# One whole value product after both score pairs, in place of two halves between them, in a fused attention kernel on one core

## What is computed

```python
def _attend(q, k, v):
    attn = jnp.einsum('bhnd,bhsd->bhns', q, k) * SCALE
    attn = jax.nn.softmax(attn, axis=-1)
    o = jnp.einsum('bhns,bhsd->bhnd', attn, v)
    ...
```

## Time and profile before

| what | value |
|---|---|
| median of 3 executions | 3727.86 us (3714.53 to 3728.5) |
| profiled execution, its own time | 3726.77 us |
| span in its trace | 3724.2 us |
| TensorE busy in the span | 3381.6 us |
| ScalarE busy | 2297.7 us |
| VectorE busy | 2203.2 us |
| mean granted TensorE clock | 0.965 |

### The profile page before, as it was taken

How to read it: one execution, slowest core, us unless ns; L and a number is a source line. 1 busy time by engine, 2 the same in 40 slices (tenths; PEclk the granted TensorE clock), 3 DMA queues, 4 the chain that set the end, 5 groups by cost and what they waited for, 6 DMA issues and landing times.

```text
span 3724.2 us, 59944 instructions
## 1 busy us (share of the span) xinstructions
PE 3381.6 (91%) x21985; PEld 1991.7 (53%) x21985; DVE 2203.2 (59%) x3645; ACT 2297.7 (62%) x3983; POOL 870.2 (23%) x578
## 2 busy tenths in 40 slices
PE   8999998898999888998898889988998899899988
PEld 6777766434644564446434744465446443564465
DVE  3323324794387456953884559636955487549654
ACT  2333333787578655875786558765874578658864
POOL 0322322103500421024103410061024100340051
PEclk8989989999999999999999999999999999999999
DMA  5011012010100001111010011100100101000100
GB/s 183 1 36 34 2 36 87 8 15 26 39 9 12 13 13 57 16 29 39 4 16 14 12 57 11 33 24 17 15 18 12 57 8 25 24 28 11 22 13 13
DMA packets 226984, 101.18 MB, mean 27 GB/s; under 512 B 159951, under 2 KB 210322, under 8 KB 226582
## 3 DMA queue, kind: packets, MB, share of 16 engines
q1 hardware_dynamic: 201734, 77.21, 8.3%
q10 hardware_dynamic: 24976, 20.15, 1.7%
HBM read 79.31 MB, written 9.96 MB: 24 GB/s over the span
## 4 chain that ended last, share of the span: by engine, by line
PE 75%; DVE 13%; ACT 7%; issue 2%; POOL 2%; DMA 1%; SPq 0%; ACTq 0%; DVEq 0%; POOLq 0%
PE ps L734 72%; DVE mxh L1789 4%; ACT probs L1468 2%; PE ps L1182 2%; DVE ctxk L1738 2%; DVE ow L1821 1%; DVE tok L1524 1%; PE ps L1043 1%; DVE small L1508 1%; DVE x L1755 1%; POOL hidl L1917 1%; DVE mx L1786 1%; ACT ow L1477 1%; ACT qs L1437 1%; POOL small L1845 1%
## 5 line engine op out<-in xcount | busy, mean ns | idle before, releaser
L1468 ACT ACTIVATE probs<-ps 128x512 f32<-128x512 f32 (+1 forms) x2176 | 1216.1, 640 | 257.0 <-PE ps L734 212.9
L1789 DVE TENSOR_REDUCE mxh<-ps 128x2 f32<-128x1024 f32 x1024 | 1217.1, 1217 | 151.8 <-PE ps L734 148.7
L734 PE MATMUL ps<-probs,v 128*32 128x256 f32 (+2 forms) x7616 | 720.9, 450 | 30.7 <-ACT ow L1477 24.4
L734 PE MATMUL ps<-ks,qs 64*128 64x512 f32 x2048 | 483.8, 481 | 63.5 <-DVE mxh L1789 34.3
L734 PE MATMUL ps<-qs,ks 64*128 64x512 f32 x2048 | 449.1, 415 | 6.7 <-DVE mxh L1789 6.1
L734 PEld LDWEIGHTS ps<-ks,qs 64*128 64x128 f32 x2048 | 192.6, 183 | 424.4 <-issue 302.9
L734 PEld LDWEIGHTS ps<-qs,ks 64*128 64x128 f32 x2048 | 250.6, 184 | 177.1 <-ACT probs L1468 150.0
L1909 POOL TENSOR_TENSOR hT<-hT,tok 128x512 f32<-128x512 f32 (+1 forms) x32 | 40.9, 1279 | 1250.5 <-DMA tok<-weights_of_outputs 1250.5
L734 PEld LDWEIGHTS ps<-probs,v 128*32 128x32 f32 (+1 forms) x7616 | 151.2, 107 | 309.1 <-ACT probs L1468 230.7
L734 PE MATMUL ps<-hT,slot 128*128 128x512 f32 x448 | 237.3, 663 | 21.4 <-issue 8.5
L1786 DVE TENSOR_REDUCE mx<-ps 128x4 f32<-128x312 f32 x384 | 165.9, 477 | 143.0 <-PE ps L734 139.7
(11 more groups left out here) (226 smaller groups left out, 5911.2 us busy)
## 6 DMA issues: line engine op xcount, KB each, us to landing
qs<-mx SPq DMA_DIRECT2D x896, 0.5 KB, 2.0
slot<-in_L_w SPq DMA_DIRECT2D x8, 1024.0 KB, 9.7
slot<-in_L_fc_w SPq DMA_DIRECT2D x8, 1024.0 KB, 5.2
hT<-ow SPq DMA_DIRECT2D x48, 128.0 KB, 2.7
tok<-weights_of_outputs SPq DMA_DIRECT2D x192, 32.0 KB, 1.8
xin<-in_x ACTq DMA_DIRECT2D x5, 1024.0 KB, 5.9
x_after_block<-x ACTq DMA_DIRECT2D x20, 256.0 KB, 2.4
xin<-x_after_block SPq DMA_DIRECT2D x5, 1024.0 KB, 5.5
```

The costliest lines, as they stand in the source:

```text
L734: return pe.matmul(out, lhsT, rhs, start=start, stop=stop)
L1468: ins = act.activation(dst, src, ACT.Exp, scale=SCALE)
L1789: dve.tensor_reduce(mxh[:, z, t, j // 2, j % 2, :], ps[:, a:a + 2, :], AX.X, ALU.max, negate=True).then_inc(dve_done, M.add(dve_done, name))
```

## The change

After the change the order within a unit that still has maxima to issue is: the first score pair, all its `A` steps, the second score pair, and then the value product of unit u - 2, whole, for every kt. Units 52 and later keep their order: first pair, whole value product, second pair. The eighth kt's product still comes at the end of its unit.

```diff
             unit = units[u - lag] if u >= lag else None
-            in_halves = unit is not None and unit[2] > 0 and taken < len(maxima)
+            maxima_first = u < end and taken < len(maxima)
+            if maxima_first:
+                more(lead + min(3 * (u + 1), 2 * (u + 1) + 4))
+                put(tag, *[("S",) + units[u] + (j,) for j in range(2, GH)])
             if unit is not None:
-                put(tag, ("PVh" if in_halves else "PV",) + unit)
-            if u < end:
-                if in_halves:
-                    more(lead + min(3 * (u + 1), 2 * (u + 1) + 4) - 1)
+                put(tag, ("PV",) + unit)
+            if u < end and not maxima_first:
                 put(tag, *[("S",) + units[u] + (j,) for j in range(2, GH)])
-            if in_halves:
-                put(tag, ("PV",) + unit)
             if unit is not None and unit[2] == NT - 1:
                 put(tag, ("O",) + unit[:2])
                 turn = unit[:2] if unit[0] == GROUPS - 1 else None
-            if u < end:
-                more(lead + min(3 * (u + 1), 2 * (u + 1) + 4))
...
-                            ins = mm(ps[32 * j:32 * j + 32, b, cs], v[0:kw, kt, GH * g + j, :],
-                                     probs[0:kw, u, j, cs], kt == 0, cross or kt == NT - 1 and kind == "PV")
-                        if kind == "PVh":
-                            continue
+                            ins = mm(ps[32 * j:32 * j + 32, b, :], v[0:kw, kt, GH * g + j, :],
+                                     probs[0:kw, u, j, :], kt == 0, cross or kt == NT - 1)
```

More of the change, by code:

```diff
@@ L296 @@
 PASS = pass_schedule()
-HALVED = {k for k in PASS if k[1] == "PVh"}
 def by_dve(tag, kind, *step):
@@ L1151, in _ @@
                             ins = mm(ps[:, b, :], ks[r, h // 2, kt * P:(kt + 1) * P], qs[r, h // 2, half])
-                    elif kind in ("PV", "PVh"):
+                    elif kind == "PV":
                         g, n, kt = step[1:]
[L1154 to L1157, removed]
+                        u = buffer_of(name)
                         b, act_was = 7, []
```

## The result

| | before | after |
|---|---|---|
| median | 3724.23 us (3714.53 to 3728.5, 4 runs) | 3792.54 us (3777.94 to 3797.19, 4 runs) |
| profiled execution, span | 3724.2 us | 3795.4 us |
| TensorE busy | 3381.6 us | 3467.9 us |
| mean granted TensorE clock | 0.965 | 0.954 |

The kernel became slower: ratio 1.018, 95% interval 1.0161 to 1.0198. The forecast was 3760 us with a range from 3735 to 3785; the time lies above it. The medians are 68.3 us apart and the two spans 71.2, since the execution of after that was profiled is the longest of its four (3797.19 us).

What follows compares the result with a forecast made beforehand. TensorE's list was taken to bound the unit at 2.475 us, DVE close behind. Terms 2.4 + 2.3 - 0.7 = 4.0 us a self attention, 32 for eight, gave 3760 us, range 3735 to 3785.

Steps and rivals of the forecast that it cites:

- A slower clock: TensorE's clock falling to its lower level at the new gaps, longest some 0.6 us; given no chance.
- The loop of the bank: Units 4 to 51: fourth score waits for the first's bank; 0.53 + 0.65 + 0.42 + 0.99 makes a unit 2.6 us.
- Copies: ACT's copies of bank 7, mid-stretch: 20.86 us apart for eight units, against 20.48 before.
- units 4 to 51: The six (g, n) of mid-stretch, +0.38 us each: 2.3 us more a self attention.
- The reductions' loop: Mid-stretch: second `A` waits for DVE to free its banks; 4.97 us for two units, 2.49 each, below 2.6.
- Unit 52: First unit without `A`: its wait for a bank of the last reductions goes, -0.7 us a self attention.
- Units 0 to 3, waits: Bank waits beside `V` in units 1 and 2, 1.9 us, and DVE waiting, 0.5: together 2.4 a self attention.
- The sum: 2.4 + 2.3 - 0.7 = 4.0 us a self attention, 32 for eight; median 3760 us.
- ends: Terms outside mid-stretch, at units 0 to 3 and unit 52: between 1 and 3 us in the range.
- Gain: Bank's wait stays hidden, units of 2.49 us: -3.6 a self attention, 3699 us; chance of over 0.5% faster 0.08.
- No change: Loop 0.05 to 0.1 us too long, or units 0 to 3 free: within 18.6 us of before; chance 0.14.
- Slower still: Bank's and DVE's waits add up instead of overlapping, unit 2.7 us: 38 us more, 3798; chance 0.08.

Runs made afterwards that it cites:

- The first experiment: New order from unit 4 on, old order in units 0 to 3, against the kernel before: 3747.01 us, ratio 1.0061.
- the fourth experiment: New order from unit 4 on, plus self-attention exponentials over 256 of 512 columns, value products reading those twice: 3699.86 us in one execution.
- the fifth: New order from unit 4 on, but value products for kt > 0 cut into two halves back to back: 3744.47 us in one execution.
- the second experiment: New order in units 0 to 3 alone, the rest as in the kernel before: 3767.2 us, ratio 1.010.

## Why the prediction went wrong

**The step that failed is the clock.** I wrote "A slower clock is no rival that I give a chance: the longest new gap is some 0.6, and with gaps of 0.52 and more the rows stand at 1.00 now." The runs show that low clock in the units 0 to 3 costs 28 us: 68 us at the lower level where the kernel before has none. Filling one of two gaps there, with nothing else changed, takes 48 of the 68 away and gives back some 21 us. The fault was in the comparison. The gap of 0.52 in the earlier trace rows comes once in 20 us of otherwise dense work. The new gaps come in units 0 to 3, where TensorE waits 1.18 for DVE already, and the next gap now follows it within a unit. I held the clock's 1.00 for an answer to how long a gap may be; it had answered that for one place. A price could have been had from the rows: a stretch of units 0 to 3 is 17.36 long, so each tenth of clock missing in it is about 1.7 an attention and 14 in the whole, and a rival at 0.8 (a level known only now) would have stood at 3788.

**The loop of the bank held.** Unit 2.61, forecast 2.6; its four terms 0.53, 0.65, 0.43, 1.00 against 0.53, 0.65, 0.42, 0.99. Copies 20.93 apart, forecast 20.86; units 4 to 51 cost 2.68, forecast 2.3, the difference being 48 units at 0.01. The first experiment shows this part alone, the fourth that it goes when only half of the bank is read, the fifth that order and not size makes it.

**The reductions' loop held too**: forecast as the next bound at 8 x 2.49 = 19.9, measured 20.03 in the fourth experiment.

**Unit 52**: forecast -0.7, measured -0.68.

**Units 0 to 3, waits**: forecast 2.4, measured 2.28, as what the other terms leave. Of its parts, 1.9 beside `V` and 0.5 for DVE, no run gives either by itself.

**The sum.** 34.2 without the clock, forecast 32: 3726.8 + 34 is 3761. On it lie 28 of clock in the units 0 to 3, which the second experiment shows together with the waits there (40.7 in all for four units of 64), and some 9 elsewhere. The range had a slip of its own: a loop of 2.65 and ends of 3 give 3.7 an attention more than the 4.0 forecast, so 3790 and not 3785; the median lies above that too.

**The rivals.** Gain fell: the bank's wait shows in every unit. No change fell. *Slower still* named a time near the true one, 3798, for another reason; its waits don't add up, since units are 2.61 and not 2.7.

**Open.** Why, of eight attentions with one list of instructions, two have 3.4 us at the lower level and three have 13.7 is not settled, nor is where the gaps must lie to bring the clock down: with `V` behind the pairs it fell in all eight, with one gap filled in five. Gaps near one another are not the whole answer either: ahead of unit 0 the kernel before waits 1.18 and then 0.60 within 2.3 us (690.76 to 693.05), at a clock of 1.00. Shown is that filling a gap took most of it away; filling both was not tried. The 9 us in the rest are mostly the clock by the estimate above, but why it was low there more often is open: each kernel was profiled in one execution, and low stretches lie elsewhere in each. The median of after rests on four runs within 19 us, which is wider than that remainder.

## What to carry to other kernels

Before a second use of a ring of banks is moved nearer to the first, write down what must pass between (here 0.53 + 0.65 = 1.18 us from score to free bank) and what the old order had there: work that seemed badly placed (half a product) was the cover, and saving 0.35 us of TensorE's work in a unit bought a wait of 0.5. A filler belongs where a bank or a copy is late, as the product between third and fourth score at kt = 0, which gave 1.1%. Where new gaps come into a stretch in which TensorE waits already, give the lower clock a price before it is held constant: the new waits here are 13.4 / 8 = 1.7 us an attention, and the clock took up to 24.1 - 19.0 = 5.1 on top.

## What the hardware showed unexpectedly

Four products more in each of two waits of an attention made the kernel some 21 us faster, at a mean clock of 0.963 against 0.954. In one attention with gaps of 1.18 and 0.45 (1836.31 to 1838.88) some 14 us at the lower level followed, in another with the same two gaps (702.41 to 704.97) 3.4 us, and the records count TensorE busy for 10.75 of 12 us of the first: a high busy share that comes from slow products, while DVE and ACT wait. At a clock of 1.00 the busy share is no better a witness: it is 123.86 of 124.10 us in units of 2.61, whose products need 2.12. And whole or cut, the float32 product costs the same to 0.04 us in eight units when its halves stand back to back and the bank is the bound.
